# VectorE's edge loop: the sum into accT placed between the two halvings

## The reference, cut to what matters

```
f    = (e @ fc_w.T).reshape(-1, 4, 128)                    # e: 100000 x 128, fc_w: 512 x 128
w    = attn[rel]                                           # one of 100 relations, 4 x 128 each
feat = sum(leaky_relu(w * f, 0.2), axis=1)                 # over the 4 heads
msg  = x[src] + feat
x    = layernorm(x + segment_sum(msg, dst, num_segments=6250))
```

## Time and profile before

| | us |
|---|---|
| three runs: median | 2623.32 |
| lowest, highest | 2622.60, 2624.45 |
| the profiled execution's span, from the first to the last instruction | 2618.1 |
| of it busy: TensorE (PE) | 2159.8 (82%) |
| VectorE (DVE) | 2255.1 (86%) |
| ScalarE (ACT) | 1740.7 (66%) |
| GpSimd (POOL) | 1919.3 (73%) |

### The profile page before, as it was taken

One profiled execution on the slowest core, in us unless ns is written; L12 is line 12 of the kernel. 1 busy time (PEld: TensorE's weight loads), 2 busy tenths in 40 slices (PEclk: granted clock), 3 DMA queues, 4 the chain that ended last, 5 costly groups with the idle time before them and its releaser, 6 DMA issues.

```text
span 2618.1 us, 44445 instructions
## 1 busy us (share of the span) xinstructions
PE 2159.8 (82%) x11261; PEld 1538.3 (59%) x11261; DVE 2255.1 (86%) x5754; ACT 1740.7 (66%) x4973; POOL 1919.3 (73%) x1845
## 2 busy tenths in 40 slices
PE   6999999999999999999999846665666666666664
PEld 3566666666666666666666535565656565556554
DVE  9999999999999999999999976666666666677887
ACT  5888888888888888888888644444444444444446
POOL 2487777777777777777777647777777777777773
PEclk8999999999999999999999877777677767777776
DMA  4233333333333333333333233333333333333343
GB/s 133 78 100 104 104 104 103 106 103 102 103 103 105 104 105 105 103 103 102 103 104 104 65 95 81 80 80 80 81 81 80 81 81 82 79 81 79 80 80 80
DMA packets 156600, 244.04 MB, mean 93 GB/s; under 512 B 40836, under 2 KB 84398, under 8 KB 156226
## 3 DMA queue, kind: packets, MB, share of 16 engines
q1 hardware_dynamic: 97730, 132.55, 17.9%
q0 software_dynamic: 58624, 108.72, 17.5%
HBM read 231.99 MB, written 9.12 MB: 92 GB/s over the span
## 4 chain that ended last, share of the span: by engine, by line
DVE 36%; issue 25%; POOL 18%; PE 7%; DMA 6%; DVEq 5%; ACT 1%; POOLq 0%; SPq 0%; ACTq 0%
POOL room L583 17%; DVE y L1231 17%; DVE hs L1239 9%; DMA room<-h_rows,y 5%; DVEq L1211 4%; DVE room L1255 4%; PE FP L986 3%; DVE accT L1215 2%; PE FP L1007 2%; PE AP L1007 1%; DVE z L1224 1%; DMA room<-h_rows,idx 1%; DVE joh L1205 1%; POOL room L591 1%; DVE room L1247 1%
## 5 line engine op out<-in xcount | busy, mean ns | idle before, releaser
L539 POOL DMA_INDIRECT room<-in_x,pk x784 | 920.7, 1174 | 262.5 <-issue 251.0
L583 POOL DMA_INDIRECT room<-h_rows,y x756 | 714.7, 945 | 235.2 <-issue 216.0
L896 PE MATMUL FP<-fc_sb,room 128*128 128x512 f32 x1568 | 832.3, 612 | 2.2 <-issue 2.2
L905 PE MATMUL WP<-at_p,rel_oh 100*128 100x512 f32 x1568 | 803.5, 594 | 0.0
L986 PE MATMUL FP<-ident,room 128*128 128x128 f32 x1664 | 342.7, 370 | 385.9 <-DMA room<-h_rows,y 351.7
L659 ACT ACTIVATE w_sb<-WP 128x512 f32<-128x512 f32 x784 | 464.1, 592 | 225.0 <-PE WP L905 219.7
L986 PEld LDWEIGHTS FP<-ident,room 128*128 128x128 f32 x1664 | 291.0, 263 | 433.3 <-DMA room<-h_rows,y 387.1
L757 ACT ACTIVATE accT<-accT,neg_big 128x512 f32<-128x512 bf16 x208 | 150.0, 722 | 559.6 <-DVE accT L1377 559.6
L905 PEld LDWEIGHTS WP<-at_p,rel_oh 100*128 100x128 f32 x1568 | 297.8, 190 | 376.5 <-issue 376.5
L1224 DVE TENSOR_TENSOR z<-FP,w_sb 128x1024 f32<-128x1024 f32 x392 | 478.6, 1221 | 1.6 <-ACT w_sb L659 1.0
L1231 DVE SCALAR_TENSOR_TENSOR y<-z 128x2048 f32<-128x2048 f32 x196 | 452.4, 2308 | 0.0
(11 more groups left out here) (246 smaller groups left out, 3181.6 us busy)
## 6 DMA issues: line engine op xcount, KB each, us to landing
room<-in_e SPq DMA_DIRECT2D x196, 256.0 KB, 2.7
rel_sb<-in_rel_g SPq DMA_DIRECT2D x196, 200.0 KB
z<-sorted_sources SPq DMA_DIRECT2D x208, 128.0 KB, 3.0
room<-in_x,pk POOLq DMA_INDIRECT x784
room<-h_rows,y POOLq DMA_INDIRECT x756
sorted_edges<-runs,spot_i POOLq DMA_INDIRECT x196, 2.0
accT<-in_x_t SPq DMA_DIRECT2D x1, 3125.0 KB, 11.2
h_rows<-arena SPq DMA_DIRECT2D x13, 227.5 KB, 2.8
```

The lines of the kernel that those rows point to most:

```text
L539: pool.indirect_dma_start(xg[:, k, u, 0:P], None, x[:, :], bass.IndirectOffsetOnAxis(ap=pk[:, g, u:u + 1], axis=0)).then_inc(xg_in[k], 16)
L583: pool.indirect_dma_start(hg[k][:, u, :], None, h_dram[:, :], bass.IndirectOffsetOnAxis(ap=sd[:, g * TG + u:g * TG + u + 1], axis=0)).then ...
L896: mm = pe.matmul(FP[u // 2][:, u % 2, :], e_sb[:, k, u, :], fc_sb[:, :], start=True, stop=True)
L905: mm = pe.matmul(WP[u % 2][:, :], rel_oh[:, k % 2, u * P:(u + 1) * P], at_p[:, j, :], start=(j == 0), stop=(j == 1))
```

## The change

On VectorE, in the edge loop, the accumulate of group g-2 moves from behind the second product z to between the two halvings hs and msg of group g-1. Operands, semaphores and every other engine's program are the same.

```diff
@@ -1261,10 +1261,11 @@
                 weigh_pair(g, k, lead, 0)
                 if prev:
                     halve(*prev)
+                if not (lead and k < 2):
+                    accumulate(g - 2, (k - 2) % SLOTS, lead)
+                if prev:
                     finish(*prev)
                 weigh_pair(g, k, lead, 1)
-                if not (lead and k < 2):
-                    accumulate(g - 2, (k - 2) % SLOTS, lead)
                 if prev:
                     add_x(*prev)
                 slope(g, k, lead)
```

## The result

| | before | after |
|---|---|---|
| median of five runs, us | 2624.45 | 2860.65 |
| lowest, highest | 2622.60, 2625.41 | 2846.38, 2870.03 |
| span of the profiled execution | 2618.1 | 2844.6 |

The ratio is 1.0899, 95% interval 1.0873 to 1.0925: the changed kernel takes 236 us more. The five runs spread over 24 us, eight times as much as before. The profiled one is the fastest of them.

A forecast was written before the change was run, and what follows sets the result against it. The prediction took VectorE and POOL, whose DMAs y holds, to bound the loop. Terms of -1.7, +213 and +10 us gave +221 on the 2618.1 us span, 2839, and 5.2 more for the median: 2844 us, range 2696 to 2934.

The forecast's parts named there:

- What bounds the loop: Edge loop: VectorE and POOL both run without waits at 7.16 us; y holds one of POOL's five DMAs per group.
- VectorE's gain of 0.14 us: VectorE per group: 0.13 saved behind the second product, 0.01 paid between hs and msg, 0.02 saved on y; 7.02 us.
- TensorE and ScalarE allow that.: Neither engine prevents 7.02 us: TensorE waits a little for the add of x, ScalarE 0.21 us and more for products.
- The edge at 7.14: POOL passes five DMAs per period only if y comes no earlier than 7.14 us behind the last y.
- How long VectorE goes on: From the loop's start VectorE keeps 7.02 us for some 12 groups, until POOL's lag of 1.76 us per group tells.
- The two paths: VectorE tied to POOL: last gather's landing to y, 3.12 us; scatter through ScalarE's copy to the first product, 5.39 us.
- The round: Slipped edge loop: y-to-y periods of 8.12 and 8.54 us in turns, mean 8.33, with holds by y and hs.
- Sum: Profiled span: -1.7 us for 12 groups, +213 for 182 groups, +10 for missed rounds; together +221, 2839 us.
- The signs: Edge loop: VectorE waits 0.5 to 1.7 us per group, two held DMAs in many groups, TensorE idles over 1 us.
- Rival 1: POOL finds a better phase, or hs holds nothing once the loop slips: 2658 to 2767 us; chance 0.19.
- Rival 2: Insertion behind hs costs 0.1 us or more, so the period stays at 7.14 or above: 2614 to 2624 us; chance 0.09.
- rival 3: The long gather is room that shrinks with the group, no hold; period 7.02 in all groups: 2596 us; chance 0.08.

The follow-up runs named there:

- after_3g: The changed kernel with three of a group's four gathers, the fourth tile's x read from the third's buffer: 2607.6 us, ratio 0.9949.
- y_reduce: The changed kernel with y as a tensor_reduce with one SBUF input and about the same length, leaky relu left out: 2607.4 us, ratio 0.9949.
- experiments 3 and 7: The changed kernel with three of four gathers, 2607.6 us; the changed kernel with y as a one-input tensor_reduce, 2607.4 us.
- Experiment 2: The kernel before, in its old order, without the accumulate's add; its register load, wait and signal stay: 2853.7 us, ratio 1.0880.
- experiment 5: The changed kernel with a useless 128x64 add on dead tiles between the second product and the add of x: 2620.9 us, ratio 0.9998.
- experiment 4, y_one_input: The changed kernel with y as a tensor_scalar with one SBUF input, stride of two elements, positive branch left out: 2606.5 us, ratio 0.9943.

## Why the prediction was right

Step by step, by its own parts.

- *What bounds the loop.* Held DMAs, not idle time, were what filled POOL. Shown by experiments 3 and 7: with a gather less, or with a y that holds nothing, the period falls to 7.11.
- *VectorE's gain of 0.14 us, period 7.02.* Measured 7.02 (116.22 to 123.24), with hs, accT and msg 1.14 and 1.27 us apart against 1.14 and 1.26. The register's load is hidden.
- *"TensorE and ScalarE allow that."* Half wrong. After about eight groups the period rose to 7.11 while VectorE's second product began to start 0.08 us late, and 7.11 is also what after_3g, y_reduce and y_one_input settle at. In these three TensorE waits for no other engine from 400 to 1400 us, though VectorE is busy for 999, 999 and 864 us of it; in the kernel before, TensorE's weight loads waited 34 us for the add of x. That speaks for TensorE as what sets 7.11. No run took work off TensorE, so it is not shown. It changed nothing in the sum, since POOL set the pace soon after.
- *The edge at 7.14.* Measured between 7.13 and 7.15. The five kernels below it (7.02 twice, 7.04, 7.11, 7.13 at the loop's start) take 2854 to 2865 us, the two above it (7.15 to 7.19, and 7.23) 2621 and 2631. Experiment 2 crosses it with the old order, experiment 5 crosses it back with the new one.
- *How long VectorE goes on.* Predicted some 12 groups; its first waits come in groups 15 (0.32 us) and 16 (1.16 us).
- *The two paths.* Both are there: ScalarE's copy into runs waits for scatters, VectorE for its copies and, less often, for gathers. The stretch from the copy to the product is 3.32 us where I had 3.34. The landings were mis-sized. I took 2.05 us for a scatter; before it was 2.0. After, the answer for line 550 from 400 to 1600 us is:

```profile
L550 POOL DMA_INDIRECT sorted_edges<-runs,spot_i x143: 924/925/2646, 401.1 to 1593.4; - x143
DMA to landing us min/median/max: 2.2/3.8/4.9
```

The median scatter is not held itself (925 ns), and still it lands late. For a gather I took 2.65 us. The add of x of one group waits for its fourth gather until 4.30 us behind the gather's start:

```profile
507.98 0.95 POOL L539 DMA_INDIRECT room<-in_x,pk  x1 [0.30 <-issue]
512.28 0.56 DVE L1255 TENSOR_TENSOR room<-room 128x384 f32<-128x384 f32 x1 [0.55 <-DMA room<-in_x,pk]
```

Why the landings are longer, no run separates; SyncE's loads of e_sb take longer too (median 3.5 us from issue to landing, 2.7 before).

- *The round.* I had 8.12 and 8.54 in turns, mean 8.33. The mean is 8.29 over the loop, 7.09 in its first 15 groups and 8.38 in the rest. The turns are not there: groups of 8.17 stand beside some of 9 to 10.8, in most of which POOL issues six or seven DMAs, and behind these often come one to three of 7.0 to 7.1 in which VectorE lives on that lead. Nor is the phase the one that I had: the scatter starts 3.5 us ahead of y in the group shown (917.79 to 921.31), not 1.9 or 2.2. The longer landing and the earlier start roughly cancel. That the number came so close is in part luck. The mechanism is not luck: POOL loses 2.1 us per group to holds (8.34 - 6.25) where it lost 0.9 before.
- *Sum.* +221 us on the span forecast, +226.5 measured for the profiled execution, 8.9 of them behind the last joh, where I had nothing. 2844 forecast, 2860.65 the median; the profiled run, 2846.38, was the fastest.
- *The signs.* VectorE's waits (1.15 us per group) are within what I named. TensorE's idle time is less, 0.8 us per group and not over 1 (busy 906 of 1000 us in 120 groups). Two held DMAs occur in many groups, as named: y holds one in 194 of the 196 groups, hs in 115.
- *Rivals.* Rival 1 (no hold by hs, or a phase that stays good) does not occur: hs holds DMAs, and the phase wanders. Rival 2 is refuted by the 1.27 us, rival 3 by the waits.

## What to carry to other kernels

Where GpSimd issues indirect DMAs beside a full VectorE, count how many of them start between two long VectorE instructions with two SBUF inputs, and how many a round needs. The count is a whole number, so a round that is a few hundredths of a microsecond too short can lose a whole DMA, and a kernel can be slower for less work. Look at the distance between a DMA's start and the holder's start in the timeline. Here 0.01 us behind y got in and 0.05 us did not, and a round of 7.13 us instead of 7.15 stood for some 240 us.

## What the runs showed of the hardware

- A VectorE instruction with two SBUF inputs holds an indirect DMA that starts behind its own start, until 2.1 to 2.2 us behind it for 2048 elements and 1.07 to 1.14 for 1024. The 128x384 add of x does the same, until 0.42 to 0.45. A tensor_reduce of 2.28 us, with one SBUF input, does not (0.94 us for the gather beside it), nor does a tensor_tensor of 1.22 us with one input in PSUM.
- One SBUF input is not always enough to let DMAs pass. The tensor_scalar of experiment 4, 1.22 us for 2048 elements, holds them until 1.1 us and more behind its start.
- The hold works in both directions, but not alike: a DMA that starts just ahead makes y 0.02 to 0.07 us longer, not 0.94.
- An indirect DMA underway is not stopped by an instruction with two SBUF inputs that starts later. The gather at 119.62 runs on for 0.94 us although hs starts at 119.77.
- A short fill behind a 128x1024 product is free (y moves by 0.02 us), an add of the same 64 columns costs 0.13 us.
- tensor_scalar on float32 took 1.22 us for 128x2048 with a stride of two elements, 0.6 ns per element and partition, half of what the forms with two inputs or a reduce need.
